# Attention with rotary latents: one matmul per head for the queries, the sine product swapped by DMA and added by POOL

## The reference, cut to what matters

```python
def _rotate_half(x):
    xe = x[..., ::2]
    xo = x[..., 1::2]
    return jnp.stack((-xo, xe), axis=-1).reshape(x.shape)
...
q_lat = q @ q2l_w.T + q2l_b
k_lat = k @ kv2l_w.T + kv2l_b
v_lat = v @ kv2l_w.T + kv2l_b
q_lat = q_lat * cos + _rotate_half(q_lat) * sin
k_lat = k_lat * cos + _rotate_half(k_lat) * sin
q_for_k = q_lat @ wqk_w.T + wqk_b
att = jnp.einsum('bhql,bhkl->bhqk', q_for_k, k_lat) * L ** (-0.5)
att = jnp.where(causal[None, None], att, -jnp.inf)
att = jax.nn.softmax(att, axis=-1)
y_lat = jnp.einsum('bhqk,bhkl->bhql', att, v_lat)
y = y_lat @ l2o_w.T + l2o_b
return y @ cproj_w.T + cproj_b
```

## Time and profile before

| | |
|---|---|
| median of 3 timed runs | 2425.71 us (2422.68 to 2427.81) |
| profiled execution | 2422.44 us, its span 2420.7 us |
| TensorE busy, of the span | 2310.3 us, 95% |
| VectorE | 1646.1 us, 68% |
| POOL | 1156.5 us, 48% |
| ScalarE | 1073.9 us, 44% |
| attention | about the first 1045 us |

### The profile page before, as it was taken

The page is one execution under the profiler, slowest core; times in us unless marked ns, Lnnn a source line. Parts: engine busy times, 40 slices in busy tenths (PEclk is TensorE's granted clock), DMA queues, the critical chain, the costliest instruction groups (busy, mean ns, idle before and its releaser), DMA issues. The chain is left out here.

```text
span 2420.7 us, 87690 instructions
## 1 busy us (share of the span) xinstructions
PE 2310.3 (95%) x35328; PEld 1553.8 (64%) x35328; DVE 1646.1 (68%) x4605; ACT 1073.9 (44%) x2707; POOL 1156.5 (48%) x1610
## 2 busy tenths in 40 slices
PE   6999999999999999869999999998999999997997
PEld 3565555556556665436666666666777777775775
DVE  3688888888877777548888888872444444443897
ACT  2656556665566666522222222222444444442444
POOL 2444454444444444337777777762333443331333
PEclk8999999999999999989999999997999999998999
DMA  2111111111111111020000000000100001101232
GB/s 86 56 36 44 45 45 45 45 45 41 45 45 45 45 45 36 28 69 27 31 30 30 30 30 26 31 22 22 35 30 30 30 30 34 31 28 46 79 87 78
DMA packets 91382, 100.88 MB, mean 42 GB/s; under 512 B 8625, under 2 KB 78033, under 8 KB 91217
## 3 DMA queue, kind: packets, MB, share of 16 engines
q1 hardware_dynamic: 91216, 98.67, 12.4%
HBM read 48.31 MB, written 33.55 MB: 34 GB/s over the span
## 5 line engine op out<-in xcount | busy, mean ns | idle before, releaser
L1427 ACT ACTIVATE r_state<-ps_state 128x64 f32<-128x64 f32 x1024 | 228.7, 223 | 335.6 <-PE ps_state L1524 330.0
L1521 PE MATMUL ps_state<-r_state,later_pairs_a 64*64 64x32 f32 x8192 | 340.9, 221 | 18.5 <-ACT r_state L1427 12.7
L1521 PEld LDWEIGHTS ps_state<-r_state,later_pairs_a 64*64 64x64 f32 x8192 | 287.6, 135 | 99.8 <-issue 81.4
L1524 PE MATMUL ps_state<-r_state,later_pairs_a 64*64 64x32 f32 x8192 | 340.9, 222 | 0.0
L399 DVE CUSTOM_DVE_ANT_0 ps_near<-ps_near,mask 128x512 f32<-128x512 f32 (+1 forms) x512 | 270.5, 590 | 92.3 <-PE ps_near L495 92.3
L273 POOL TENSOR_SCALAR_AFFINE_SELECT probsT<-probsT 128x512 f32<-128x512 f32 x256 | 159.4, 635 | 315.3 <-ACT probsT L382 173.6
L1524 PEld LDWEIGHTS ps_state<-r_state,later_pairs_a 64*64 64x64 f32 x8192 | 284.8, 135 | 0.0
L399 DVE CUSTOM_DVE_ANT_0 ps_far<-ps_far,mask 128x384 f32<-128x384 f32 (+1 forms) x512 | 198.8, 461 | 47.4 <-PE ps_far L495 46.4
L1234 PE MATMUL ps_down<-kept_w_downT,f_hT 128*128 128x256 f32 (+1 forms) x768 | 190.5, 390 | 1.9 <-ACT f_hT L1146 1.9
L1141 ACT ACTIVATE f_silu<-ps_gate 128x704 f32<-128x704 f32 x64 | 48.5, 757 | 313.8 <-PE ps_gate L1226 310.3
L503 PE MATMUL ps_far<-Q,K 32*128 32x256 f32 (+2 forms) x1536 | 175.8, 414 | 0.7 <-ACT probsT L379 0.5
(11 more groups left out here) (209 smaller groups left out, 5368.1 us busy)
## 6 DMA issues: line engine op xcount, KB each, us to landing
k_swap<-k_sin SPq DMA_DIRECT2D x128, 128.0 KB, 2.0
xT<-in_xT_dram SPq DMA_DIRECT2D x16, 512.0 KB, 3.6
xtok<-in_x_dram SPq DMA_DIRECT2D x16, 512.0 KB, 3.8
x_rows<-x SPq DMA_DIRECT2D x16, 512.0 KB, 2.8
f_x<-x_rows SPq DMA_DIRECT2D x64, 128.0 KB, 2.0
x_rows<-f_x SPq DMA_DIRECT2D x64, 128.0 KB, 1.7
r_x<-x_rows SPq DMA_DIRECT2D x64, 128.0 KB, 2.0
x_rows<-r_x SPq DMA_DIRECT2D x64, 128.0 KB, 1.9
```

The source lines that it names most:

```text
L1427: nc.scalar.activation(state[:, j % 2, banks, :, t, 0, :], sums[:, j % 2, banks, :, now], ACT.Tanh).then_inc(state_ready[t], 1)
L1521: nc.tensor.matmul(sums[half(v), j % 2, stays, c, now], A[half(v), 3 * q, c, :], last[half(v), stays, c, :], start=False, stop=True, skip_ ...
L1524: out = nc.tensor.matmul(sums[half(1 - v), j % 2, changes, c, now], A[half(v), 3 * q + 1 + was, c, :], last[half(v), changes, c, :], start ...
```

## The change

The four matmuls per group with the swapped wqk go. Instead SP swaps neighbouring partitions of q_sin with two DMAs into a new tile q_swap, POOL adds q_swap to q_cos, and one set of four matmuls multiplies the sum by wqk. VectorE makes q_sin first and then q_cos, each with its own increment of `q_turned`. SP does the queries' swap ahead of the keys' swap; POOL does the queries' addition between the keys' cosine product and the keys' addition. TensorE's block is now latent queries, latent keys, queries; the queries wait for POOL's addition (`q_added`), which belongs to the cycle before.

```diff
@@ sync
+                def swap_latent(b, g):
+                    s = (g + 1) % 2
+                    sp.wait_ge(q_turned, cyc(2, b, g, 7))
+                    for i in range(2):
+                        sp.dma_start(q_swap[i:P:2, s, :], q_sin[1 - i:P:2, s, :]).then_inc(q_swapped[s], 16)
...
+                        if runs(i, g, 3):
+                            swap_latent(i, g)
                         if runs(i, g, 2):
                             swap(i, g)
@@ gpsimd
+                def add_latent(b, g):
+                    m = GROUPS * b + g + 3
+                    s = m % 2
+                    pool.wait_ge(q_turned, 2 * m + 2)
+                    pool.wait_ge(q_swapped[s], 32 * (m // 2 + 1))
+                    nc.gpsimd.tensor_tensor(q_cos[:, s, :], q_cos[:, s, :], q_swap[:, s, :], ALU.add).then_inc(q_added, 1)
...
                     nc.gpsimd.tensor_tensor(mine, mine, cos_t, ALU.mult).then_inc(k_cos_ready, 1)
+                    if runs(b, g, 3):
+                        add_latent(b, g)
                     pool.wait_ge(k_swapped[s], 64 * b + 32 * ((g + 2) // 2 + 1))
...
                         if runs(i, g, 2):
                             turn_keys(i, g)
+                        elif runs(i, g, 3):
+                            add_latent(i, g)
@@ vector
-                            nc.vector.scalar_tensor_tensor(q_cos[:, s, :], far[3], q2l_b, cos_t, ALU.add, ALU.mult)
                             nc.vector.scalar_tensor_tensor(q_sin[:, s, :], far[3], q2l_b, sin_t, ALU.add, ALU.mult).then_inc(q_turned, 1)
+                            nc.vector.scalar_tensor_tensor(q_cos[:, s, :], far[3], q2l_b, cos_t, ALU.add, ALU.mult).then_inc(q_turned, 1)
@@ tensor
-                def query(s, part):
-                    source = (q_cos, q_sin)[part]
+                def query(s):
                     for t in range(GROUP):
-                        out = nc.tensor.matmul(far[1][rows_of(t), :], w_qf[rows_of(t + 1), part, :], source[rows_of(t + 1), s, :],
-                                               start=(part == 0), stop=(part == 1), skip_group_check=True)
-                    return out
+                        out = nc.tensor.matmul(far[1][rows_of(t), :], w_qf[rows_of(t + 1), :], q_cos[rows_of(t + 1), s, :],
+                                               start=True, stop=True, skip_group_check=True)
+                    out.then_inc(Q_full, 1)
...
+                    if runs(i, g, 3):
+                        pe.wait_ge(q16_out, 2 * i + {0: 2, 1: 3, 2: 3, 3: 4}[g])
...
+                        latent(far[3], 0, q16, g3, 1, q_full)
                     if runs(i, g, 2):
-                        pe.wait_ge(q_turned, cyc(1, i, g, 3))
...
-                        query(g % 2, 0)
                         pe.wait_ge(k16_out, 2 * i + (2 if g < 2 else 3))
...
                         latent(far[2], 1, k16, g2, 0, K_full)
-                    if runs(i, g, 3):
...
-                        latent(far[3], 0, q16, g3, 1, q_full)
-                    if runs(i, g, 2):
-                        query(g % 2, 1).then_inc(Q_full, 1)
+                        pe.wait_ge(q_added, cyc(1, i, g, 3))
...
+                        query(g % 2)
...
                             elif t == 3 and runs(i, g, 3):
-                                pe.wait_ge(q_turned, cyc(1, i, g, 4))
+                                pe.wait_ge(q_turned, cyc(2, i, g, 8))
```

More of the change, by code:

```diff
@@ L100, in attention @@
         w_lat = sb("w_lat", [P, 4, LATENT])
-        w_qf = sb("w_qf", [P, 2, LATENT])
+        w_qf = sb("w_qf", [P, LATENT])
         reps = sb("reps", [LATENT, 2, P])
@@ L119, in attention @@
         q_sin = sb("q_sin", [P, 2, SEQ])
+        q_swap = sb("q_swap", [P, 2, SEQ])
         k_sin = sb("k_sin", [P, 2, SEQ])
@@ L155, in attention @@
         k_swapped = [sem(f"k_swapped{s}") for s in range(2)]
-        q_full, q_turned = sem("q_full"), sem("q_turned")
+        q_full, q_turned, q_added = sem("q_full"), sem("q_turned"), sem("q_added")
+        q_swapped = [sem(f"q_swapped{s}") for s in range(2)]
         Q_full, Q_out = sem("Q_full"), sem("Q_out")
@@ L612, in cycle @@
                         out.then_inc(yt_full, 1)
-                    if runs(i, g, 2):
-                        pe.wait_ge(q_turned, cyc(1, i, g, 3))
[L617 to L622, removed]
-                        query(g % 2, 0)
+                    if runs(i, g, 3):
+                        pe.wait_ge(q16_out, 2 * i + {0: 2, 1: 3, 2: 3, 3: 4}[g])
+                        if is_cycle(i, g, -2) or is_cycle(i, g, -1):
+                            pe.wait_ge(q_turned, cyc(2, i, g, 6))
+                        elif is_cycle(i, g, 0):
+                            pe.wait_ge(topped, 12)
+                        elif runs(i, g, -1):
+                            await_cycles(pe, exped, 12, i, g - 1, 12)
+                        latent(far[3], 0, q16, g3, 1, q_full)
+                    if runs(i, g, 2):
                         pe.wait_ge(k16_out, 2 * i + (2 if g < 2 else 3))
@@ L631, in cycle @@
                         latent(far[2], 1, k16, g2, 0, K_full)
-                    if runs(i, g, 3):
-                        pe.wait_ge(q16_out, 2 * i + {0: 2, 1: 3, 2: 3, 3: 4}[g])
-                        if is_cycle(i, g, -2) or is_cycle(i, g, -1):
-                            pe.wait_ge(q_turned, cyc(1, i, g, 3))
+                        pe.wait_ge(q_added, cyc(1, i, g, 3))
+                        if is_cycle(i, g, -1):
+                            pe.wait_ge(Q_out, 1)
                         elif is_cycle(i, g, 0):
-                            pe.wait_ge(topped, 12)
+                            pe.wait_ge(topped, 8)
                         elif runs(i, g, -1):
-                            await_cycles(pe, exped, 12, i, g - 1, 12)
-                        latent(far[3], 0, q16, g3, 1, q_full)
-                    if runs(i, g, 2):
-                        query(g % 2, 1).then_inc(Q_full, 1)
+                            await_cycles(pe, exped, 12, i, g - 1, 10)
+                        query(g % 2)
                     if runs(i, g, 0):
@@ L799, in attention_arrays @@
     wqk_t = f("wqk_w").T
-    swapped = wqk_t.reshape(LATENT // 2, 2, LATENT)[:, ::-1, :].reshape(LATENT, LATENT)
     w_lat = np.zeros((P, 4, LATENT), np.float32)
@@ L810, in attention_arrays @@
                             [np.tile(f(name), P // f(name).size) for name in ("q2l_b", "kv2l_b", "l2o_b", "wqk_b")], 1),
-        "w_lat": w_lat, "w_qf": np.tile(np.stack([wqk_t, swapped], 1), (GROUP, 1, 1)),
+        "w_lat": w_lat, "w_qf": np.tile(wqk_t, (GROUP, 1)),
         "reps": np.stack([np.tile(f("kv2l_w"), (1, 8)), np.tile(f("l2o_w").T, (1, 8))], 1),
```

## The result

| | before | after |
|---|---|---|
| median of the timed runs | 2426.22 us (2422.68 to 2427.81, 4 runs) | 2401.63 us (2400.83 to 2406.75, 4 runs) |
| ratio of the runs | | 0.9915, 95% interval 0.9896 to 0.9934 |
| profiled execution, its span | 2422.44, 2420.7 us | 2406.75, 2405.0 us |
| first to last of the 62 blocks (61 cycles) | 50.77 to 985.25: 934.48 us | 51.06 to 969.60: 918.54 us |
| what follows attention | 1043 to 2420 us | 1027 to 2405 us |

The kernel became faster, by more than the forecast of 2416 and just beyond its range (2403 to 2424). The two spans differ by 15.7 us; 15.9 are won between the first and the last block, 0.3 are lost ahead of the first, and the three later stages are unchanged. (The last block has no latent queries in the new order; its keys start at 969.63, and T is put 0.03 ahead of them, as in the other cycles.)

What follows compares the result with a forecast made beforehand. TensorE was taken to bound attention, 954.2 of 960 us busy. Terms -13.3 + 2.5 + 1.0 = -9.8 us gave 2412.6 on the profiled execution, 2415.9 on the median, forecast 2416; own range 2408 to 2421, wider range 2403 to 2424.

Steps and rivals of the forecast that it cites:

- TensorE's saving: In each attention block, dropping the second query product's eight passes brings the turned scores 0.75 us earlier, at T+1.10.
- the far banks' copies: Tile 2 scores must wait for ScalarE and VectorE to free the far banks, so TensorE newly stands still 0.46 us or more.
- the swaps: Two added DMAs per cycle on SP's queue, ahead of the key swap: landed at T+4.6, cost 0.
- the keys' addition: On POOL, behind the new 1.27 us addition: ends about 0.3 later, at T+7.6, wanted at T+11.1, cost 0.
- VectorE's release: End of VectorE's two query products: T+2.77 before, about T+2.67 after, as latent queries start 0.13 earlier.
- Rival (c): Slower: the latent keys' set waits for the latent queries' set, 0.58 us a cycle, +36 us, 2461; chance 0.06.
- Rival (b): TensorE keeps most of its 0.75 because copies start earlier than read: half to all of 46.5 us, 2379 to 2402; chance 0.08.
- Q only follows K; neither gets earlier: ScalarE's copy of Q waits only for its copy of K, which hangs on the latent keys; Q still ends at T+2.68.
- the term of 0.25 a cycle: Attention cycle's net gain, within bounds 0.10 and 0.29; over 53 cycles 13.3 us saved.
- nine cycles that gain nothing: In 9 cycles TensorE already waits for VectorE's row maxima behind a long weight quantisation piece, so a shorter block gains nothing.
- the side cost on VectorE: POOL's new addition blocks a quantiser tensor_scalar at the shared port: bounds 0 and 10.2 us for all 8, 2.5 taken.
- What the start costs: Queries' swap and addition stand ahead of the first keys' on SP and POOL: bounds 0 and 2.4 us, 1 taken.

Runs made afterwards that it cites:

- e4: The changed kernel without the two swap DMAs and POOL's new addition, the queries' sine part left out; 2405.82 us, ratio 0.9928 to the kernel before.
- e6: The kernel before without the four sine-part matmuls, in its own old order, sine part left out; 2411.95 us, ratio 0.9951 to the kernel before.
- e7: e4 with VectorE's unused sine product cut to 16 columns; 2398.15 us, ratio 0.9896 to the kernel before.
- e5: The kernel before with only TensorE's block reordered: latent queries, latent keys, cosine part, sine part; 2432.78 us against 2422.68, ratio 1.0043.
- e1: The changed kernel unaltered, run again on another chip; 2408.71 us against 2421.38 for the kernel before, ratio 0.9944.
- e10: The changed kernel unaltered, run again in a third set; 2405.04 us against 2421.84 for the kernel before, ratio 0.9927.
- e2: The changed kernel with POOL's addition of the queries put behind the keys' addition; 2412.35 us, ratio 0.9961 to the kernel before.

## Why the prediction was right or wrong

**Right: the place and the mechanism.** TensorE's saving is 0.73 (0.75 said), the turned scores come at T+1.12 (T+1.10), the far banks' copies decide, and most of the saving is given back (0.43 of 0.73). K's copy, the swaps, the keys' addition and the later stages are where they were put. VectorE's release moved by 0.16, to T+2.61 (0.10, to T+2.67). Rival (c) is out: the keys' set did not wait. Rival (b), copies that start earlier than I read, is what happened to one of the two, but it brought 0.30, not half of 0.75.

**Wrong: "Q only follows K; neither gets earlier".** This is the step that failed, and with it the term of 0.25 a cycle, which measured 0.30. In the kernel before Q's copy did not follow K: it waited for the sine part, the very thing that was removed. e4, e6 and e7 have it at T+1.87 without that part, e5 moves it to T+2.11 with it. The trace of before held the sign. K's copy ends at 417.52 + 0.69 = 418.21, and Q's starts at 418.25, 0.04 behind the earlier trace rows. On VectorE the first product is

```profile
417.62 0.75 DVE L441 SCALAR_TENSOR_TENSOR q_cos<-ps_far,columns,cos_sin 128x512 f32<-128x512 f32 x1 [0.53 <-PE ps_far L522]
```

and ends at 418.37, but the next one starts at 418.29: two operations that really follow each other overlap by 0.08. ScalarE's pair after overlaps by 0.11 (411.30 + 0.69 = 411.99 against 411.88). A gap of 0.04 is a wait of about 0.12 to 0.15. The Trainium skill (Perfetto Trace Analysis, "Per-instruction lifecycle: what the profiler-reported window actually captures") says that a recorded duration of VectorE or ScalarE ends when the write is acknowledged, while the next instruction may begin to fetch before that; the overlaps of 0.08 and 0.11 agree.

So Q is out 0.13 earlier and q_cos 0.16. I had the waiting heads go at T+2.74 to T+2.83, which with the old T+3.03 gave 0.20 to 0.29; they go at T+2.60 (412.62) and T+2.66 (412.68). The later one is 0.37 ahead of T+3.03, and 0.31 of that arrives at the values (T+4.03 to T+3.72): the overheads for which I took 0.25 instead of 0.29 exist, about 0.06, but they came off a larger number. Both releases had to move for this: had Q's copy stayed at T+2.68, the same 0.06 would leave 0.23 a cycle (an estimate), and with VectorE's left at T+2.79 e6 has 0.13.

**Wrong: nine cycles that gain nothing.** The earlier trace rows counts waits, and I read them as cycles. The nine waits lie in six cycles: two each in 2, 3 and 60, one each in 20, 25 and the last. Of these only 20 and 25 have any quantisation on VectorE. Cycle 2 has none:

```profile
86.14 0.30 PEld L503 LDWEIGHTS ps_far<-Q,K 32*128 32x128 f32 x6 [0.20 <-DVE top L399]
86.81 0.18 PEld L503 LDWEIGHTS ps_far<-Q,K 32*128 32x128 f32 x1 [0.37 <-DVE top L399]
```

and it gained 0.47. Nor is it enough that quantisation stands behind the query products: it does so in every cycle from 4 to 41, and nearly all of them gained 0.30. What matters is which piece. The one of L906, L908 and L910 stands there in the cycles 11, 20, 25, 30 and 39; four of them, all but 25, give the gain back (0.32 each, e4). In 6, 15 and 34 the same piece follows z's addition, and the gain stays. Cycle 29, with another piece, gives back 0.2. Why 25 does not and 29 does was not followed up.

**Right: the side cost on VectorE.** POOL's addition on VectorE: 2.5 said; e4 gives 2.0 to 3.1 for the addition and the swaps together. It came where it was put: L930 took 1396 ns at most after, from 434, in two of its eight times (the cycles 20 and 30; in e1 also in 25, in e10 also in 11).

```profile
L930 DVE TENSOR_SCALAR weights_power<-weights_power x8: 434/436/1396, 146.4 to 643.0; 128x528 f32<-128x528 f32 x8
```

That it would lie nearer to 10.2 than to 0, as the prediction has it in one place, did not come out: only five of the eight pieces stand there, and two or three of them met the addition. What the start costs, 1 by the forecast, cannot be told: against the first of the 62 blocks before (50.77), it lies 0.3 later here, 0.5 earlier in e1, 0.1 later in e10, and 0.8 later in e4, which has neither the swaps nor the addition.

**The sum by its terms**, from the periods of the 61 cycles: 61 x (-0.30) = -18.3; -1.0 more in the cycles 0, 2, 3, 7 and 10, which gained up to 0.55; +1.3 for four cycles bound by VectorE; +1.9 for POOL's addition in 20 and 30; +0.2 in 29; +0.3 at the start: -15.6, and the span fell by 15.7. Forecast: -13.3 + 2.5 + 1.0 = -9.8. Of the 5.9 between them, 4.7 are the first term (-18.3 - 1.0 + 1.3 = -18.0 against -13.3): 53 x 0.05 = 2.7 by the size of the cycle's gain, the other 2.0 by the cycles that I had left out. Why the cycles 7 and 10 gain 0.55 was not followed up.

The larger part of the distance between forecast and result lies elsewhere. Taken off the 2425.7 that I started from, 15.7 would have given 2410, inside my own range (2408 to 2421), and with the differences of e1 and e10, 12.7 and 16.8, it would have been 2413 and 2409. The 24.6 between the medians hold 8.9 more: 5.1 between the traced execution after and its median, 3.8 between the one before and its median. The clocks on record (0.980 against 0.982 after) and the two other sets of runs speak for the clock of the single executions; as the clocks of before on the first chip are missing, this part is argued and not shown.

## What to carry to other kernels

When a part is removed, ask of every reader in the trace whether it was waiting for that part, and decide "follows its predecessor" against "waited a little" by the pitch of pairs that surely run back to back on that engine, not by the gap to the recorded end. Two consumers within 0.1 us of each other are both the bound: removing work ahead of one is worth only the distance to the other, and an order that loses alone (e5) may win once the part is gone. An operation added to POOL is priced by what VectorE does at that moment, down to its smallest operations, and moving it moves that price.

## What the runs showed of the hardware

A product or sum of POOL with two operands in SBUF can hold a VectorE operation of 128x16 until it ends: 1.88 us instead of 0.20 (e2). I had thought only of the long pieces. The Trainium skill (SBUF — State Buffer, "Who interferes with whom") says that whoever takes the shared port pair first keeps it for the whole instruction; the release at 422.50, 0.06 behind POOL's end, agrees, and shows that a tiny operation pays as much as a long one.

VectorE can get in between two operations of POOL: in cycle 20, L928 and L930 each took 1.40 us, ending 0.29 behind the end of a POOL product (351.52 + 1.48 = 353.00) and 0.29 behind that of the addition (354.43), and POOL's addition itself took 1.47 instead of 1.27. It looks as if each side waited for the other in turn; no experiment took this apart.

Two single-bank copies of 128x512 on ScalarE start 0.58 us apart though each is recorded with 0.68 to 0.69; on VectorE the pitch is 0.66 with 0.74 to 0.75 recorded.
